# Softmax maxima from pieces of 370 keys with a third bank for score tiles, in an attention and expert-layer kernel

## The reference

```python
q = lat @ Wq                                   # 2 x 1024 queries, 16 heads x 64
k, v = split(concat([x, lat], axis=1) @ Wkv)   # 2 x 1101 keys
dots = einsum('bhid,bhjd->bhij', q, k) * 64 ** -0.5
attn = softmax(dots, axis=-1)                  # over 1101 keys
x = x + einsum('bhij,bhjd->bhid', attn, v) @ Wout
# then x = x + shared FFN + routed experts (32 experts, top 4 of the groups chosen)
```

## Time and profile before

| what | us |
| --- | --- |
| time, median of 3 runs | 1699.55 (1697.3 to 1701.94) |
| the profiled execution: its own time | 1705.26 |
| its span on the core | 1703.5 |
| TensorE busy | 1545.7 (91%) |
| VectorE busy | 1050.0 (62%) |
| ScalarE busy | 795.4 (47%) |
| GpSimd busy | 939.5 (55%) |

### The profile page before, as it was taken

How to read it: one execution, slowest core, us unless ns; L and a number is a source line. 1 busy time by engine, 2 the same in 40 slices (tenths; PEclk the granted TensorE clock), 3 DMA queues, 4 the chain that set the end, 5 groups by cost and what they waited for, 6 DMA issues and landing times.

```text
span 1703.5 us, 23797 instructions
## 1 busy us (share of the span) xinstructions
PE 1545.7 (91%) x8086; PEld 1075.3 (63%) x8086; DVE 1050.0 (62%) x1576; ACT 795.4 (47%) x1499; POOL 939.5 (55%) x749
## 2 busy tenths in 40 slices
PE   3899999999999989799999889996889999999995
PEld 2565565555555645455555555544778999999995
DVE  6556557666575576766656766555745666666662
ACT  3355345444544554334454434533325666666663
POOL 4467656666676666466877556784422343433433
PEclk8899999999999999899999999988898999999998
DMA  3033430000000000000010000102226676666664
GB/s 99 12 77 81 105 77 14 10 14 10 23 14 10 23 14 10 14 10 24 29 37 24 10 14 20 34 17 81 75 90 175 177 193 167 185 178 169 193 168 93
DMA packets 99282, 117.93 MB, mean 69 GB/s; under 512 B 10595, under 2 KB 78181, under 8 KB 99173
## 3 DMA queue, kind: packets, MB, share of 16 engines
q1 hardware_dynamic: 82149, 96.97, 19.5%
q0 software_dynamic: 17056, 19.97, 6.0%
HBM read 74.93 MB, written 35.06 MB: 65 GB/s over the span
## 4 chain that ended last, share of the span: by engine, by line
PE 76%; DVE 14%; ACT 5%; issue 2%; POOL 2%; DMA 1%; SPq 0%; ACTq 0%; DVEq 0%; POOLq 0%
PE ps_o L830 14%; PE ps_t L690 9%; PE ps_m L792 8%; PE ps_m L690 8%; PE ps_st L690 8%; PE ps_st L815 7%; PE ps_st L819 6%; DVE arena_r L1185 3%; PE ps_t L850 3%; ACT arena L1443 3%; PE ps_m L727 3%; PE ps_o L727 2%; PE ps_t L895 2%; DVE arena_r L1174 1%; PE ps_t L798 1%
## 5 line engine op out<-in xcount | busy, mean ns | idle before, releaser
L635 POOL TENSOR_TENSOR arena<-arena 128x512 f32<-128x512 f32 (+1 forms) x512 | 660.8, 1292 | 387.6 <-ACT arena L1443 351.3
L1443 ACT ACTIVATE arena<-ps_st 128x512 f32<-128x512 f32 (+1 forms) x576 | 327.8, 596 | 497.5 <-PE ps_st L819 453.3
L1185 DVE TENSOR_REDUCE arena_r<-ps_m 128x1 fp32r<-128x1101 f32 x256 | 332.6, 1299 | 214.8 <-PE ps_m L792 210.3
L665 POOL DMA_INDIRECT acc_rows<-arena,ids x96 | 150.7, 1570 | 292.3 <-ACT arena L1504 264.6
L815 PE MATMUL ps_st<-arena_r 128*128 128x512 f32 (+1 forms) x576 | 267.0, 464 | 27.2 <-ACT arena L1443 27.1
L830 PE MATMUL ps_o<-arena 128*64 128x512 f32 (+1 forms) x1152 | 269.9, 603 | 0.0
L819 PE MATMUL ps_st<-arena_r 68*128 68x512 f32 (+2 forms) x576 | 234.7, 407 | 16.3 <-DVE arena_r L1192 16.3
L792 PE MATMUL ps_m<-arena_r 128*128 128x512 f32 (+1 forms) x768 | 196.9, 366 | 28.9 <-DVE arena_r L1185 24.1
L792 PEld LDWEIGHTS ps_m<-arena_r 128*128 128x128 f32 x768 | 138.0, 196 | 125.3 <-DVE arena_r L1185 56.0
L815 PEld LDWEIGHTS ps_st<-arena_r 128*128 128x128 f32 (+1 forms) x576 | 108.8, 189 | 114.4 <-ACT arena L1443 84.0
L690 PE MATMUL ps_m<-arena_r 128*128 128x320 f32 (+1 forms) x864 | 166.7, 329 | 1.3 <-DVE arena_r L1307 1.2
(11 more groups left out here) (171 smaller groups left out, 1866.2 us busy)
## 6 DMA issues: line engine op xcount, KB each, us to landing
arena<-in_L_ffn_wg_dram SPq DMA_DIRECT2D x32, 512.0 KB, 4.6
arena<-in_L_ffn_wu_dram SPq DMA_DIRECT2D x32, 512.0 KB, 6.3
arena<-in_L_ffn_wd_dram SPq DMA_DIRECT2D x32, 512.0 KB, 3.9
x_slots<-route SPq DMA_DIRECT2D x5, 2176.0 KB, 12.9
arena<-x_slots SPq DMA_DIRECT2D x32, 272.0 KB, 2.6
arena_r<-arena_r SPq DMA_DIRECT2D x30, 275.2 KB, 3.8
arena<-in_L_xattn_Wkv_dram SPq DMA_DIRECT2D x32, 128.0 KB, 2.4
arena<-x_slots SPq DMA_DIRECT2D x32, 68.0 KB, 2.4
```

The lines of the kernel that those rows point to most:

```text
L635: pool.tensor_tensor(total, probsT[0:rows, h, 0, :] if kt == 1 else total, probsT[0:rows, h, kt, :], ALU.add).then_inc(added, 1)
L665: pool.indirect_dma_start(out=dst[:, :], in_=y_sb[par][:, c, 0:w], in_offset=None, compute_op=ALU.add, out_offset=bass.IndirectOffsetOnAxi ...
L1185: dve.tensor_reduce(neg[h][:, c:c + 1], scores_m[:, 0:KEYS], AX.X, ALU.max, negate=True)\
L1443: act.activation(probsT[0:rows, h, kt, :], ps_st[0:rows, n % 2, :], ACT.Exp).then_inc(exp_done, 1)
```

## The change

The maxima of a half are made in six steps (`MAX_STEPS`) in place of four. The 1101 keys are cut into three pieces of 369 that overlap by a few keys (starts 0, 366 and 732; the matmul takes 370 columns, the reduction 369). Four query tiles by three pieces are twelve pieces, two to a step. A step is two matmuls of 370 columns, each into a bank of its own, and one reduction of [128, 2, 369] to two columns. A seventh VectorE event (`neg`) reduces the 4 x 3 piece maxima to the four negated maxima, and `row` waits for it. `ps_m` shrinks to two banks and still holds one step: TensorE waits before each step for the reduction of the step before. `ps_st` grows to three banks: a tile waits for the exponential of tile n - 3. The hand-written order has the six steps spread over other slots.

```diff
-        own_max = [own("max", d, 1, i) for i in range(4)]
-        next_max = [nxt("max", n, 0, i) for i in range(4)]
+        own_max = [own("max", d, 1, i) for i in range(MAX_STEPS)] + [own("neg", d, 1)]
+        next_max = [nxt("max", n, 0, i) for i in range(MAX_STEPS)] + [nxt("neg", n, 0)]
...
-        after = {(0, 8): [own("row", d, 1), old("sum", prev)],
-                 (1, 1): [],
-                 (1, 2): [old("norm", prev), next_max[0]],
-                 (1, 3): first_values + [next_max[1]]}
+        after = {(0, 1): own_max[1:2],
+                 (0, 4): own_max[4:5],
+                 (0, 6): own_max[5:],
+                 (0, 8): [own("row", d, 1), old("sum", prev)],
+                 (1, 1): next_max[0:1],
+                 (1, 2): [old("norm", prev), next_max[1]],
+                 (1, 3): first_values + [next_max[2]],
+                 (1, 4): [out[0], next_max[3]]}
         if project:
-            after[0, 0] = [own_max[0]] + project_k(0) + [own_max[1], k_low[0]]
+            after[0, 0] = [own_max[0]] + project_k(0)
+            after[0, 1] += [k_low[0]]
             after[0, 2] = project_k(2) + [own_max[2], k_low[2]]
-            after[0, 3] = project_k(1) + [k_low[1]]
-            after[0, 5] = project_q() + [q_again] + last_values + [q_low, own_max[3]]
-            after[1, 4] = [out[0], next_max[2]]
-            after[1, 5] = [nxt("v", pp, 0), next_max[3]]
-            after[1, 6] = more_values + [nxt("row", n, 0), out[1]]
+            after[0, 3] = project_k(1) + [own_max[3], k_low[1]]
+            after[0, 5] = project_q() + [q_again] + last_values + [q_low]
+            after[1, 5] = [nxt("v", pp, 0), next_max[4]]
+            after[1, 6] = next_max[5:] + more_values + [nxt("row", n, 0), out[1]]
...
         else:
-            after[0, 0] = [own_max[0]] + project_q() + [own_max[1]]
-            after[0, 3] = [own_max[2]]
-            after[0, 5] = [q_again] + last_values + [q_low, own_max[3]]
-            after[1, 4] = [out[0], next_max[2]]
-            after[1, 6] = [out[1], next_max[3]] + more_values + [nxt("row", n, 0)]
+            after[0, 0] = [own_max[0]] + project_q()
+            after[0, 2] = [own_max[2]]
+            after[0, 3] = [own_max[3]]
+            after[0, 5] = [q_again] + last_values + [q_low]
+            after[1, 5] = [next_max[4]]
+            after[1, 6] = next_max[5:] + [out[1]] + more_values + [nxt("row", n, 0)]
...
-                    pe.wait_ge(max_done, T * MAX_T + d * 8 + h * 4 + i + 1)
-                    c = d % 2 * 512 + i * P
-                    for lo, w in ((0, 512), (512, 512), (S, CT + 1)):
-                        mm = pe.matmul(scores_m[:, lo:lo + w], q1[h][:, c:c + P], k1[pp][h][:, lo:lo + w],
+                    pe.wait_ge(max_done, T * MAX_T + (d * 2 + h) * MAX_STEPS + i + 1)
+                    for bank_m, piece in enumerate((2 * i, 2 * i + 1)):
+                        c = d % 2 * 512 + piece // KEY_PIECES * P
+                        lo = piece % KEY_PIECES * PIECE
+                        mm = pe.matmul(ps_m[:, bank_m, 0:PIECE_W + 1], q1[h][:, c:c + P], k1[pp][h][:, lo:lo + PIECE_W + 1],
                                        start=True, stop=True)
...
-                    dve.tensor_reduce(neg[h][:, c:c + 1], scores_m[:, 0:KEYS], AX.X, ALU.max, negate=True)\
-                       .then_inc(max_done, 1)
+                    dve.wait_ge(max_ready, T * MAX_T + (d * 2 + h) * MAX_STEPS + i + 1)
+                    dve.tensor_reduce(piece_max[:, :, :].rearrange("p a k -> p (a k)")[:, 2 * i:2 * i + 2],
+                                      ps_m[:, :, 0:PIECE_W], AX.X, ALU.max).then_inc(max_done, 1)
+                if kind == "neg":
+                    _, d, h = ev
+                    dve.wait_ge(max_done, T * MAX_T + (d * 2 + h + 1) * MAX_STEPS + 1)
+                    c = MROW[h].start
+                    dve.tensor_reduce(neg[h][:, c:c + 4], piece_max[:, :, :], AX.X, ALU.max, negate=True)\
+                       .then_inc(neg_done, 1)
```

More of the change, by code:

```diff
@@ L44 @@
 HIDS = 4
+MAX_STEPS = 6
+KEY_PIECES = 3
 def turn_slots():
@@ L97, in turn_slots @@
         else:
-            after[0, 0] = [own_max[0]] + project_q() + [own_max[1]]
-            after[0, 3] = [own_max[2]]
-            after[0, 5] = [q_again] + last_values + [q_low, own_max[3]]
-            after[1, 4] = [out[0], next_max[2]]
-            after[1, 6] = [out[1], next_max[3]] + more_values + [nxt("row", n, 0)]
+            after[0, 0] = [own_max[0]] + project_q()
[4 more added lines that the diff above has]
+            after[1, 6] = next_max[5:] + [out[1]] + more_values + [nxt("row", n, 0)]
         if d == 0:
-            after[1, 1] = [own("w", 1)]
+            after[1, 1] = [own("w", 1)] + after[1, 1]
         if d == 2:
-            after[1, 1] = [(("w", 0), -1)]
+            after[1, 1] = [(("w", 0), -1)] + after[1, 1]
         for h in range(2):
@@ L160, in whole_plan @@
               ("hi", "k", 0, 1, (0, 1)), ("bstat", 1), ("lo", "k", 0, 1), ("max", 0, 0, 0), ("v", 0, 0),
-              ("max", 0, 0, 1), ("v", 0, 1), ("max", 0, 0, 2), ("v", 0, 2), ("max", 0, 0, 3), ("row", 0, 0)]
+              ("max", 0, 0, 1), ("max", 0, 0, 2), ("v", 0, 1), ("max", 0, 0, 3), ("max", 0, 0, 4), ("v", 0, 2),
+              ("max", 0, 0, 5), ("neg", 0, 0), ("row", 0, 0)]
     plan = [(ev, 0) for ev in before]
@@ L249, in xattn_moe @@
     O_T = QUADS
-    MAX_T = O_T * 8
+    MAX_T = O_T * 2 * MAX_STEPS
+    NEG_T = O_T * 2
+    PIECE = -(-(KEYS - 1) // KEY_PIECES) // 2 * 2
+    PIECE_W = KEYS - (KEY_PIECES - 1) * PIECE
+    assert PIECE_W >= PIECE and PIECE_W % 2 == 1 and 2 * MAX_STEPS == 4 * KEY_PIECES and PIECE_W < 512
     ST_T = O_T * 2 * KT_N
@@ L374, in xattn_moe @@
         sq_junk = sb("sq_junk", [GE, D])
+        piece_max = sb("piece_max", [P, 4, KEY_PIECES])
         carries = sb("carries", [P, E])
@@ L814, in _ @@
                     pe.wait_ge(exp_done, T * ST_T + n + 1)
-                    pe.matmul(ps_st[0:rows, n % 2, :], k1[pp][h][:, r], q1[h][:, c:c + 512],
+                    pe.matmul(ps_st[0:rows, n % 3, :], k1[pp][h][:, r], q1[h][:, c:c + 512],
                               start=True, stop=False)
@@ L818, in _ @@
                         job_done(pe, JOB[("row", d, h), T])
-                    pe.matmul(ps_st[0:rows, n % 2, :], k2[pp][h][kr, r], q2[h][kr, c:c + 512],
+                    pe.matmul(ps_st[0:rows, n % 3, :], k2[pp][h][kr, r], q2[h][kr, c:c + 512],
                               start=False, stop=True).then_inc(st_ready, 1)
@@ L1345, in _ @@
             act.sem_inc(ysb_ready, 2)
-            act.sem_inc(exp_done, 2)
+            act.sem_inc(exp_done, 3)
             act.wait_ge(consts, 1)
@@ L1442, in _ @@
                     act.wait_ge(st_ready, T * ST_T + n + 1)
-                    act.activation(probsT[0:rows, h, kt, :], ps_st[0:rows, n % 2, :], ACT.Exp).then_inc(exp_done, 1)
+                    act.activation(probsT[0:rows, h, kt, :], ps_st[0:rows, n % 3, :], ACT.Exp).then_inc(exp_done, 1)
                 if kind == "ws":
```

17 lines of the change are left out of this document (7 added, 10 removed).

## The result

The changed kernel takes **1842.05 us** (median of 4 runs, 1841.56 to 1842.92) where the kernel before takes 1698.75 (4 runs): ratio **1.083**, 95% interval 1.0815 to 1.0853, or 143 us slower. The profiled execution took 1841.56 us, its span is 1839.8, and the mean granted clock is 0.951 (before 0.967).

The account below looks back on a forecast made before the run. TensorE, busy 91%, was taken as the bound: new waits of 218 us, less gains of 18 and 43 and further corrections, make 143; with 23 for the clock, 166, so 1865 us (+9.8%), range 1765 to 1915.

Parts of the forecast that it names:

- Behind the reciprocal: Every block: the second next-block step waits for the reduction queued behind VectorE's reciprocal, 2.61 us lost with the late start.
- The weight split: Blocks d = 0 and 2: VectorE's weight split between reciprocal and reduction adds 1.15 us to the wait there.
- the step's gain: Every half: six steps of 0.34 us in place of four totalling 2.32, 0.28 us less, 18 us over 64 halves.
- The terms for the `lo` differences: First half with key projection: differences between VectorE's reductions cost 0.2 at the third step, 0.8 fifth, 0.2 held bank.
- The third bank, 43 us: Score tiles: a third bank removes 79 waits of TensorE for exponentials, at 0.54 us each, 43 us gained.
- The clock: Longer idle behind the reciprocal lowers TensorE's clock in 18 of 31 blocks, 1.28 us a fall, 23 us.
- That only the wait at the reciprocal is real: Rival: single tiles cover the short reductions and only the wait behind the reciprocal costs; +50, 1750 us; chance 0.12.
- Falls at 47 waits: Rival: the clock falls at nearly every new wait, 47 times in place of 18, 1902 up to 1940 us; chance 0.12.
- The faster case: Rival: new waits only replace time TensorE would be held up by ScalarE and GpSimd; 1638 us; chance 0.04.
- A: Theory: TensorE waits for the one `ps_m` behind single tiles and behind the reciprocal, and these waits also lower the clock.
- B: Rival theory: one of the two waits, behind single tiles or behind the reciprocal, carries nearly all of the loss.
- C: Rival theory: TensorE would lose the time anyway, and taking a wait away only moves it to a later one.

Follow-up runs that it names:

- One bank a piece: Changed kernel with each matmul of a step waiting only for its own bank's reduction, twelve reductions a half: 1799.7 us, ratio 1.059.
- matmuls in the wait: Changed kernel plus eight unused 512-column matmuls ahead of the step that waits behind the reciprocal: 1815.3 us, ratio 1.066.
- the own steps apart: Changed kernel with the own half's second to fifth maximum steps set apart in blocks d = 0 and 2: 1838.2 us, ratio 1.080.
- the 129 us of the order: Changed kernel reordered so no step stands behind a single tile, `av` groups split: 1713.0 us, ratio 1.008.
- splitting the buffer (35 us): Third order, next-block steps off the reciprocal, `av` groups whole: 1694.8 us with one-bank pieces, 1729.4 us with two-bank steps.
- the second experiment: Changed kernel with the next block's maximum steps one place later, the first off the reciprocal: 1778.2 us, ratio 1.044.

## Why the prediction was right, and where its sizes were off

The range and the mechanism held; 1865 was 23 us above the measured 1842. That it came so near is partly luck: by the estimates below the waits were put some 27 us too high and the clock some 10 us too low. By steps:

- **Reduction and step.** 0.92 us, matmuls 0.17 apart and 0.61 for two behind a wait, all as predicted; the cycle is 1.63 us to the hundredth. One bank a piece, which leaves the order as it is and only shortens the wait for the buffer, gave back 42 us.
- **First half without key projection, and `row`.** Three losses of 0.71, 0.82 and 0.82 us for the forecast 0.82 each and, before `row`, 0.37 us of idle ("about 0.4") stand where they were put.
- **Behind the reciprocal.** Forecast 2.61 us; without weight split 2.47 + 0.1 measured. Moving the steps away gave the second halves 85 us back, with weight split and falls of the clock in it. Right.
- **The weight split, mis-sized.** Forecast 1.15 us more in blocks d = 0 and 2; behind the reciprocal it takes 0.62 with 0.08 overlap, so 0.54. The mean of 1.24 hid a wide spread at this same place: 0.615 to 2.900 us with a median of 0.868 in the trace before, 0.615 to 1.703 with a median of 0.690 after. In eight of the sixteen blocks the reduction follows 0.54 us behind its start, as here. Net of the smaller steps (0.56) and of four bank waits of 0.54, the forecast for such a block is 8.43 - 0.56 - 2.16 = 5.7 us; measured without a fall 34.24 - 29.2 = 5.0. The weight split is about the difference.
- **Blocks with key projection: the step's gain, mis-sized.** The forecast for the block is 5.20 - 0.56 - 1.08 (two bank waits in the trace before, one in each half) = 3.6 us; measured without a fall 39.1 - 36.07 = 3.0. The first half lost 0.7 us (forecast 0.95), the second 2.3 (2.6). The terms for the `lo` differences stand where they were put. In the first half of the block at 110 us the fifth step starts 0.94 us behind the tile's second matmul in place of 0.23 and takes 0.45 in place of 0.34, 0.82 lost (forecast 0.8); the third loses 0.28 (0.2), and a bank held by a late difference 0.23 more than before (0.2). What was too small is the gain of the smaller step. The prediction read the old one behind a tile, 0.51; behind a projection or an `av` group it took 0.61, the new one behind a projection 0.34. Timeline of TensorE before, behind a projection:

```profile
87.07 0.77 PE L792 MATMUL ps_m<-arena_r 128*128 128x512 f32 x3
87.68 0.47 PE L815 MATMUL ps_st<-arena_r 128*128 128x512 f32 x1
```

  If the two plain blocks stood for all, both mis-sizes together are 16 x (0.7 + 0.5), an estimate of 19 us.
- **The third bank, 43 us: right as a sum, wrong as a cause.** The waits for ScalarE went as counted, 24.7 us of idle to 0.7, and the blocks' sums come out with 0.54 a wait. But undoing the bank costs 6 us (not clear of the noise) and not 43: the new waits for VectorE, which the prediction itself counted, give ScalarE the time. The step that failed is "I count all 43" as a gain of the bank. Where the new waits are away, undoing it costs 12 us.
- **The clock, mis-sized the other way.** Forecast 18 more falls at 1.28, 23 us; measured 22 more, at 1.35 us (matmuls in the wait) to 1.65 (the twelve `av` matmuls), so 30 to 36 us. The Trainium skill ("TensorE: Matmul & The Clock Gate", HAM oscillation) says that waits of 3 to 5 us for transfers between bursts make each burst start cold. The trace of the changed kernel agrees in most blocks and not in each, with waits of mostly 2.3 to 2.9 us for VectorE: four of 31 have a wait behind the reciprocal and no fall, one of them (it ends at 618.59) of 2.89 us, as long as those that have one. The same page's section on a second failure mode says that short idles in frequent turn do it too; the three idles of 0.56 us at 500.50 to 503.76 agree, the same three in the changed kernel don't.
- **Routing blocks.** The two d = 2 blocks with routing (40.1 us before, one fall each already) lost 1.7 us each and not 5.7: 8 us of the excess.
- **Rivals.** That only the wait at the reciprocal is real fell with the cycle of 1.63 us and the 42 us of one bank a piece. Falls at 47 waits fell: there are 22 more than before. The faster case fell: the waits cost far more than the gains.

Of the theories of the experiments A holds. B falls: off the reciprocal alone 64 us come back, one bank a piece alone 42, and only an order without both waits comes near the time before. C is true of two cases: for the own steps apart the thing that took the gain is the clock, and of what the third bank saves in the first halves a part is lost again in the second, where `out` waits longer for GpSimd. Open stay two things: whether GpSimd's wait is the whole of what took the third bank's gain there, and how the 129 us of the order divide, since that edit moved the steps, `row` and the `av` groups at once.

## What to carry to other kernels

With a single PSUM buffer, the work from one refill's start to the next must last longer than refill, reduce and release (1.63 us here): count it for every pair of neighbours when the order or the size of steps changes, and splitting the buffer (35 us) may do more than a smaller step. Don't place a step whose reader stands behind a long operation ahead of work that other engines wait for. A gain ahead of a wait that lowers the clock can be lost there: the same edit was worth 4 us, hardly clear of the noise, and then 23 once the wait was filled.

## What the runs showed of the hardware that wasn't expected

- The clock fell after a run of three idles of 0.55 to 0.56 us with some 1.1 us of work between (503.76 in the second experiment), in four first halves of sixteen, and in three of the kernel with the matmuls in the wait; in the changed kernel it didn't after the same run. A single idle of 1.53 us had left it at 1.00, and so did one of 2.89 us in the changed kernel (window 618.60 to 622.00), where equal ones in other blocks lowered it. So the length of one idle doesn't decide it alone. What a fall cost differed as well: 1.35 to 1.65 us behind the reciprocal, 1.6 to 3.1 us behind the run of three.
- A `ps_m` step or a single `av` group placed between matmuls of the other number format (fp32r and fp32) took longer than inside a run of its own. Timeline of TensorE in the kernel with the own steps apart:

```profile
287.39 1.08 PE L844 MATMUL ps_o<-arena 128*64 128x512 f32 x4
288.40 0.61 PE L806 MATMUL ps_m<-arena_r 128*128 128x370 f32 x2
288.85 0.39 PE L829 MATMUL ps_st<-arena_r 128*128 128x512 f32 x1
...
290.42 0.60 PE L806 MATMUL ps_m<-arena_r 128*128 128x370 f32 x2
290.94 1.08 PE L844 MATMUL ps_o<-arena 77*64 77x512 f32 x4
291.95 0.50 PE L829 MATMUL ps_st<-arena_r 128*128 128x512 f32 x1
```

  Four `av` matmuls take 1.01 us to the next start, twelve in one run of the changed kernel 2.73 (0.91 for four), and the steps beside them 0.45 and 0.52 in place of 0.34. The rows show the price beside the change of format. The 0.45 is no proof of it, since a step behind a wait takes 0.45 too (288.94 to 289.39 in the changed kernel); a run that holds all else equal wasn't made.
